# Attention scores for the row maximum from an fp32r copy of the queries and keys that ScalarE makes

## The reference

```
h = layernorm(x)
q, k, v = h @ Wq.T, h @ Wk.T, h @ Wv.T        # 16 query heads, 4 key/value heads, 8 wide
q, k = rotary(rms_norm(q)) * q_gain, rotary(rms_norm(k))
att = softmax(mask(q @ k.T / sqrt(8)))        # each query sees itself and the 31 tokens before it
x = x + mix_pairs(att @ v) @ Wo.T
h = layernorm(x)
logits = h @ router_w.T                       # 8 experts, the best two of each token, gated by
                                              # two softmaxes with a jitter threshold
x = x + sum over the two of w_e * (silu(h @ w_gate[e].T) * (h @ w_up[e].T)) @ w_down[e].T
```

## Time and profile before

| what | value |
|---|---|
| median of three runs | 566.21 us (562.92 to 570.49) |
| the profiled execution, first to last instruction | 673.3 us |
| TensorE busy in it | 550.8 us (82%) |
| ScalarE busy in it | 370.5 us (55%) |
| mean granted TensorE clock | 0.918 |

### The profile page before, as it was taken

How to read it: one execution, slowest core, us unless ns; L and a number is a source line. 1 busy time by engine, 2 the same in 40 slices (tenths; PEclk the granted TensorE clock), 3 DMA queues, 4 the chain that set the end, 5 groups by cost and what they waited for, 6 DMA issues and landing times.

```text
span 673.3 us, 23426 instructions
## 1 busy us (share of the span) xinstructions
PE 550.8 (82%) x7519; PEld 473.6 (70%) x7519; DVE 424.6 (63%) x1700; ACT 370.5 (55%) x1170; POOL 345.8 (51%) x536
## 2 busy tenths in 40 slices
PE   3899999999999999987657669888887878887860
PEld 1578887777878777875537569777787778776850
DVE  5788898898989988883554226355444454544452
ACT  4467776666757766651246437455554555554530
POOL 3333346667776666763343381435455444556355
PEclk9999999999999999995756779899899899999895
DMA  7333333233332222222111223334444443443333
GB/s 215 67 72 74 71 81 96 65 82 82 69 72 46 53 45 53 53 48 62 33 54 44 65 67 96 99 114 135 115 120 126 111 123 102 126 122 107 103 107 82
DMA packets 126310, 58.20 MB, mean 86 GB/s; under 512 B 54000, under 2 KB 121712, under 8 KB 126192
## 3 DMA queue, kind: packets, MB, share of 16 engines
q1 hardware_dynamic: 117424, 39.03, 23.3%
q0 software_dynamic: 8192, 16.79, 8.6%
q10 hardware_dynamic: 576, 0.88, 0.4%
HBM read 28.15 MB, written 24.58 MB: 78 GB/s over the span
## 4 chain that ended last, share of the span: by engine, by line
PE 69%; another core or an unknown queue 9%; issue 8%; ACT 5%; DMA 3%; DVE 2%; POOL 2%; SPq 1%; ACTq 1%; POOLq 0%; DVEq 0%
PE chb L727 16%; PE pv L581 7%; PE chb L639 6%; PE pm L592 5%; PE pp L752 5%; PE pp L661 5%; PE pv L752 4%; PE chb L630 4%; PE chb L626 3%; PE tp L744 2%; PE tp L684 2%; POOL ga L1368 2%; PE tp L554 2%; PE tp L560 2%
## 5 line engine op out<-in xcount | busy, mean ns | idle before, releaser
L1368 POOL DMA_INDIRECT ga<-expert_out,row_all x128 | 122.3, 955 | 137.1 <-DVE yb L1257 83.9
L1297 POOL DMA_INDIRECT expert_in<-xn,slot_r x128 | 126.9, 992 | 121.5 <-DVE slot_r L921 96.5
L727 PE MATMUL chb<-xbT,wcur 128*128 128x128 f32 x1144 | 162.4, 288 | 0.0
L727 PEld LDWEIGHTS chb<-xbT,wcur 128*128 128x128 f32 x1144 | 150.6, 205 | 0.0
L1250 DVE TENSOR_TENSOR hT<-sil,chb 128x256 f32<-128x256 f32 x143 | 60.1, 420 | 114.2 <-ACT sil L507 86.3
L507 ACT ACTIVATE sil<-chb 128x256 f32<-128x256 f32 x143 | 54.9, 384 | 124.2 <-PE chb L727 57.2
L417 ACT ACTIVATE pT<-chb 128x512 f32<-128x512 f32 x128 | 77.1, 602 | 69.8 <-PE chb L639 59.5
L938 DVE TENSOR_REDUCE mx<-chb 128x8 f32<-128x512 f32 x128 | 86.7, 685 | 18.0 <-PE chb L639 13.9
L524 ACT COPY wcur<-wgu 128x512 f32 x143 | 89.9, 629 | 5.6 <-issue 5.3
L744 PE MATMUL tp<-ident,xb 128*128 128x128 f32 x143 | 42.5, 297 | 48.9 <-issue 38.6
L581 PEld LDWEIGHTS pv<-vext,pT 128*64 128x64 f32 x1984 | 68.1, 140 | 13.8 <-issue 13.3
(11 more groups left out here) (140 smaller groups left out, 1051.1 us busy)
## 6 DMA issues: line engine op xcount, KB each, us to landing
xb<-expert_in SPq DMA_DIRECT2D x143, 64.0 KB
expert_out<-yb SPq DMA_DIRECT2D x71, 128.0 KB
xa<-x SPq DMA_DIRECT2D x16, 256.0 KB
out<-oo SPq DMA_DIRECT2D x31, 128.0 KB
qk<-qk SPq DMA_DIRECT2D x64, 48.0 KB
wgu<-w_gu SPq DMA_DIRECT2D x16, 128.0 KB
expert_in<-xn,slot_r POOLq DMA_INDIRECT x128
ga<-expert_out,row_all POOLq DMA_INDIRECT x128
```

The lines of the kernel that those rows point to most:

```text
L727: last = nc.tensor.matmul(chb[:, b % 4, n * P:(n + 1) * P], wcur[:, b % 3, n * P:(n + 1) * P], xbT[:, b % 4, :], start=True, stop=True)
L1297: nc.gpsimd.indirect_dma_start(xs_dram, bass.IndirectOffsetOnAxis(ap=slot_r[:, q % 4, 2 * v + k:2 * v + k + 1], axis=0), xn2[:, t % 16, :] ...
L1368: nc.gpsimd.indirect_dma_start(ga[:, q % 2 * TPS + v, j, :], None, ys_dram[0:min(blocks, LIVE) * P, :], bass.IndirectOffsetOnAxis(ap=row_a ...
```

## The change

ScalarE gets one more instruction per tile: it copies the tile's `qk` (128x384, float32) into a new buffer `qkr` of type fp32r with two slots. The four score products for the row maximum (L630) read `qkr` in place of `qk`; the scores that go into the exponential still read `qk` in float32. TensorE's waits for VectorE's transpose (`tr_ok`) and for the transfers (`kp_in`) before `attend` go to ScalarE, in front of the copy, and TensorE waits for the copy (`qkr_ok`). The copy stands after the second normalised tile and ahead of the cast of the maxima.

```diff
--- before.py
+++ after.py
@@ -178,7 +178,7 @@
         t12, t3 = sb("t12", [P, 4, 2, RF]), sb("t3", [P, 4, RF])
         tq = sb("tq", [P, 4, QF + KV * (KF + HD)])
         vtok, vext = sb("vtok", [P, 8, KF]), sb("vext", [P, 8, CH, VX])
-        qk = sb("qk", [P, 8, 3 * P])
+        qk, qkr = sb("qk", [P, 8, 3 * P]), sb("qkr", [P, 2, 3 * P], F32R)
         mx, stm = sb("mx", [P, 4, CH, WIN]), sb("stm", [P, 4, P], F32R)
         pT = sb("pT", [P, 4, CH, 2 * P])
         rec = sb("rec", [P, HEADS])
@@ -240,7 +240,7 @@
         t3_ok, t4_ok, tr_ok = sem("t3_ok"), sem("t4_ok"), sem("tr_ok")
         kp_in = [sem(f"kprev_in{n}") for n in range(8)]
         scores_done, max_ok, tm_done, stm_ok = sem("scores_done"), sem("max_ok"), sem("tm_done"), sem("stm_ok")
-        exp_ok, pv_done, y_ok, ones_ok = sem("exp_ok"), sem("pv_done"), sem("y_ok"), sem("ones_ok")
+        qkr_ok, exp_ok, pv_done, y_ok, ones_ok = sem("qkr_ok"), sem("exp_ok"), sem("pv_done"), sem("y_ok"), sem("ones_ok")
         wo_done, x2_ok, xn2_ok, lg_done = sem("wo_done"), sem("x2_ok"), sem("xn2_ok"), sem("lg_done")
         lg_read, dd_ok, ee_ok, both_ok = sem("lg_read"), sem("dd_ok"), sem("ee_ok"), sem("both_ok")
         rank_done, rank_read, slot_ok = sem("rank_done"), sem("rank_read"), sem("slot_ok")
@@ -471,6 +471,13 @@
                     wait(act, scat[q % 4], q // 4 * TPS * 2 * 16)
                     nc.scalar.activation(xn2[:, t % 16, :], xa[:, t, :], ACT.Identity, scale=rs2[:, q % 2, v:v + 1],
                                          bias=nb2[:, q % 2, v:v + 1]).then_inc(xn2_ok, 1)
+
+                t = tile(s, L_S)
+                if t is not None:
+                    act.wait_ge(tr_ok, t + 1)
+                    act.wait_ge(kp_in[t % 8], kprev_total(t))
+                    wait(act, scores_done, scores(t - 2 + L_S))
+                    nc.scalar.copy(qkr[:, t % 2, :], qk[:, t % 8, :]).then_inc(qkr_ok, 1)
 
                 t = tile(s, L_MAX)
                 if t is not None:
@@ -611,8 +618,7 @@
                 wait(pe, max_ok, 2 * upto(s, L_MAX))
                 wait(pe, exp_ok, 2 * upto(s, L_EXP))
                 if a is not None:
-                    pe.wait_ge(tr_ok, a + 1)
-                    pe.wait_ge(kp_in[a % 8], kprev_total(a))
+                    pe.wait_ge(qkr_ok, a + 1)
                 if b is not None:
                     pe.wait_ge(stm_ok, b + 1)
                 rows = [slice(c * WIN, (c + 1) * WIN) for c in range(CH)]
@@ -627,7 +633,7 @@
                                             start=True, stop=False, skip_group_check=True)
                 if a is not None:
                     for c in range(CH):
-                        last = nc.tensor.matmul(chb[:, c, 0:2 * P], qk[rows[c], a % 8, 0:P], qk[rows[c], a % 8, P:3 * P],
+                        last = nc.tensor.matmul(chb[:, c, 0:2 * P], qkr[rows[c], a % 2, 0:P], qkr[rows[c], a % 2, P:3 * P],
                                                 start=False, stop=(b is None), skip_group_check=True)
                 if b is not None:
                     for c in range(CH):
```

## The result

The changed kernel takes **578.5 us** at the median of four runs (576.66 to 582.19) against 564.7 us for the kernel before (562.92 to 570.49). The ratio is **1.0274**, 95% interval 1.0242 to 1.0306: slower by 2.7%. The forecast was 578 us. That the number fits so well is partly luck: four of its terms were off, and their errors largely cancel. It also started from a median of three runs, 566.2 us, which is 1.5 us above that of four, so the forecast rise was 12 us and the measured one is 13.8. The experiments show which terms were off.

The account below looks back on a forecast made before the run. TensorE was taken to set the attention step of 4.33 us. 48 x 0.15 + 16 x 0.43 gave 14 us, 9.6 without holds; taking 12, 566.2 + 12 = 578 us, range 567 to 588.

Parts of the forecast that it names:

- TensorE's bound before, and the loop: Attention: TensorE sets the 4.33 us step; waiting for ScalarE's copy closes a loop through both engines, 4.48 us undisturbed.
- The copy: ScalarE's new instruction per tile: 0.51 us, with 0.47 and 0.63 us for the ends.
- From exponentials to normalised tile: ScalarE's row in an undisturbed step: exponentials at 1.25 us, second normalised tile at 3.53 us, waiting for the projection between.
- The four products: TensorE's products for the maximum in fp32r: 0.22 us instead of 0.44, so 0.22 us less per tile.
- A: Start of the mask products in a step; exponentials forecast 1.25 instead of 1.47 us after it.
- The hand-over: From the end of ScalarE's copy to TensorE's start: 0.05 us, taken from L430.
- The rival of a single pass: The four fp32r products take 0.11 us, undisturbed steps cost 0.04 us more: 573 us, chance 0.07.
- The holds: Exponentials delayed, 1.19 us in one step, while GpSimd issues an indirect transfer; 16 such steps cost 0.43 us more each.
- What I costed at nothing: Cast of the maxima behind the copy, and waits for VectorE and transfers moved to ScalarE: no cost, up to 3 us.
- The signs: Trace signs: 4.48 us steps, 0.51 us copy ending 0.05 us before mask products, TensorE idle there, late-exponential steps of 5.4 us.
- The likeliest case: The loop through ScalarE's copy closes in attention: 578 us, between 572 and 586, chance 0.74.

Follow-up runs that it names:

- the copy alone: The changed kernel with the four products for the maximum reading float32 queries and keys again, copy and wait kept: 598.3 us, ratio 1.0618.
- the exchange: The changed kernel with ScalarE's copy moved ahead of the second normalised tile: 562.8 us, ratio 1.0009 to the kernel before.
- the products last: The changed kernel with the four fp32r products and the wait for the copy moved behind the other score products: 553.5 us, ratio 0.9816.
- the second profile: The kernel before, unchanged, profiled once more: span 561.8 us, mean step 4.38 us, median 563.1 us.
- copy-early run: The changed kernel with the copy moved up in ScalarE's row, right behind the second exponentials: 577.8 us, ratio 1.0290.

## Why the prediction was right, point by point

**TensorE's bound before, and the loop.** Right, and shown from both sides. Taking 0.31 us out of the loop on TensorE (the fp32r products against the copy alone) shortens the step by 0.31; taking 0.39 us out of it on ScalarE (the exchange) shortens it by 0.38; taking the need for the copy out of it altogether (the products last) leaves TensorE's 4.02.

**The copy** at 0.51 us: 0.508 in the trace. **From exponentials to normalised tile**: 2.28 forecast, 2.30 measured, with the wait for the projection in it as forecast.

**The four products** at 0.22 us less: the wrong size, 0.30 to 0.31. The row of L634 was not the price of its own products. Of that, 0.29 shows between A and the exponentials: 1.18 us, where I had 1.25. **The hand-over** at 0.05 us: the wrong size, 0.22. I took it from L430, where one wait stands in front of the instruction; here another stands behind it. The errors partly cancel: -0.07 for the exponentials, +0.02 for the normalised tile and +0.17 for the hand-over make 0.12, and the step is 4.60 instead of 4.48. The rival of a single pass had the products right and the outcome wrong (a step of 4.37, 573 us), since it took the same hand-over.

**The holds**: wrong. I had given 16 steps of 0.43 us to them because one profile showed them, with a warning that this profile was 107 us too long. In the second profile the loop's mean step is only 0.05 above 4.33, and the changed kernel has no late exponential. Sixteen held steps at 0.43 instead of 0.15 made the sum 14 instead of 9.6, and I had gone to the middle, so some 2.4 of the forecast's 12 us were for holds.

**What I costed at nothing**: the start. That waits in the first steps keep TensorE's clock down was not in the sum, although the prediction looked at the clock in the middle of the loop. The first nine steps are a third of the loss between the two profiled executions (6.3 of 18.6 us); the run that leaves the first eight tiles uncopied wins 2.9 to 5.5 us back. The cast of the maxima and the transfers stayed covered, as said: TensorE's transposes and ScalarE's copy hardly ever waited for them.

**The signs.** TensorE's idle time ahead of the mask products, the copy of 0.51 us and the gap between 60 and 100 us came as named. The 0.22 us between the weight loads of the four products and the next group came too, as 0.20, but does not measure those products. Three others did not come: the copy ends 0.22 us ahead of the mask products, the profile names the cast and not the copy, and there are no steps of 5.4 us with a late exponential. Four products at 0.11 us were also to show that I was wrong; they came, and the loop held all the same: a badly chosen sign.

So the sum of the forecast was 64 x 0.15 plus about 2.4 for holds; the measured one is 50 x 0.22 in the loop plus 6 in the start. The likeliest case was the right one, in its mechanism; that its size was right is luck.

## What to carry to other kernels

When a step of one engine is made to wait for an instruction at the end of another engine's row, look for the closed loop, and add up everything in it, hand-over too; the engine with the shorter work can then set the pace without ever being busy all the time. The cure is seldom to make the added instruction shorter: ask for it later (behind work that does not need it) or put it ahead of work that is not in the loop, and look first which second loop it would enter. A row used as the price of an operation must have the same neighbours: the start of a weight load tells when it was issued, not when its own products ran. And the releaser that a profile names for a wait is the semaphore that came last by its reckoning; look in the program whether it can be the one.

## What the runs showed of the hardware

- Four fp32r products 32 rows deep with 256 columns save 0.30 to 0.31 us against float32 ones at the upper clock level, of 0.44 us. With 0.28 us of idle time ahead of them, it takes 0.11 us from their first weight load to that of the next group.
- The hand-over from a ScalarE copy to TensorE took 0.05 us with one wait directly ahead of the products, 0.12 with the wait last in a row of four, 0.22 with one more wait behind it; the wait instructions themselves stand 0.11 us apart in the trace.
- Idle time of 1.1 and 1.3 us ahead of the mask products in the first steps went with TensorE staying at 1.2 GHz until 43 us instead of 26 us. In the copy-early run, idle time of 2.0 us in the middle of the loop was followed by 6.8 us at 1.2 GHz.
- One profiled execution of an unchanged kernel was 112 us longer than another, with waits of its own.
